# A convolution unit's banks read in halves, and the moments of the finished tiles in three pieces

## The reference, cut to what matters

```python
def _L1_xattn_ref(k, v, q, ssm_kernel, D, head_dim):     # k = v = ctx, q = layernorm(x)
    B, HD, L = k.shape
    H = HD // head_dim                                   # 32 heads of 8
    k_ = k.reshape(B, H, head_dim, L)
    v_ = v.reshape(B, H, head_dim, L)
    q_ = q.reshape(B, H, head_dim, L)
    kv = jnp.einsum('bhil,bhjl->bijhl', k_, v_)
    kv_f = jnp.fft.rfft(kv, n=fft_size)
    kernel_f = jnp.fft.rfft(ssm_kernel, n=fft_size)
    y = jnp.fft.irfft(kv_f * kernel_f, n=fft_size)[..., :L]
    out = y + kv * D[None, None, None, :, None]
    out = jnp.einsum('bijhl,bhil->bjhl', out, q_)
...
x = x + _L1_xattn_ref(ctx_2048, ctx_2048, _layernorm(x, axis=-1), L1_xattn_ssm_kernel, L1_xattn_D, 8)
x = x + _L1_ffn_ref(_layernorm(x, axis=-1), ...)
```

## Time and profile before

| | us |
|---|---|
| median of 3 timed runs | 2039.91 |
| lowest and highest | 2039.51, 2041.14 |
| the profiled execution | 2046.15 |
| its span | 2044.30 |
| TensorE busy in the span | 1912.9 (94%) |
| VectorE | 1396.4 (68%) |
| ScalarE | 802.7 (39%) |
| GpSimd | 641.8 (31%) |
| granted clock of TensorE, mean | 0.959 |

### The profile page before, as it was taken

One profiled execution on the slowest core, in us unless ns is written; L12 is line 12 of the kernel. 1 busy time (PEld: TensorE's weight loads), 2 busy tenths in 40 slices (PEclk: granted clock), 3 DMA queues, 4 the chain that ended last, 5 costly groups with the idle time before them and its releaser, 6 DMA issues. The chain is left out here.

```text
span 2044.3 us, 35178 instructions
## 1 busy us (share of the span) xinstructions
PE 1912.9 (94%) x13798; PEld 1629.1 (80%) x13798; DVE 1396.4 (68%) x2817; ACT 802.7 (39%) x1484; POOL 641.8 (31%) x507
## 2 busy tenths in 40 slices
PE   5799999999999999999999996999989989988997
PEld 3588888888888888999999995776777687767886
DVE  7778888888887866555555552788866847784554
ACT  5545555555455533122222212444534443232332
POOL 2433443333333330000000001776755620002553
PEclk6799999999999999999999997999999978998999
DMA  4211211111222133323223214535443443324774
GB/s 153 87 62 64 73 63 63 63 63 74 73 72 81 46 112 99 110 94 104 89 98 104 93 63 157 183 109 168 146 124 113 134 174 117 124 83 145 179 179 61
DMA packets 111752, 214.66 MB, mean 105 GB/s; under 512 B 14243, under 2 KB 34787, under 8 KB 110563
## 3 DMA queue, kind: packets, MB, share of 16 engines
q1 hardware_dynamic: 104194, 195.30, 28.4%
q0 software_dynamic: 7392, 17.11, 4.1%
HBM read 136.11 MB, written 76.34 MB: 104 GB/s over the span
## 5 line engine op out<-in xcount | busy, mean ns | idle before, releaser
L1415 PE MATMUL psum<-kv,toep 128*128 128x288 f32 x1280 | 328.3, 419 | 40.5 <-ACT yx L1463 24.3
L1415 PEld LDWEIGHTS psum<-kv,toep 128*128 128x128 f32 x1280 | 249.3, 196 | 117.0 <-ACT yx L1463 30.4
L168 PE MATMUL psum<-xn_t_h,w_gate_h 128*128 128x256 f32 x768 | 232.9, 303 | 1.3 <-DVE xn_th L293 1.3
L168 PE MATMUL psum<-xn_t_h,w_up_h 128*128 128x256 f32 x768 | 217.6, 283 | 0.0
L169 PE MATMUL psum<-xn_t_l,w_up_h 128*128 128x256 f32 x768 | 217.5, 283 | 0.0
L170 PE MATMUL psum<-xn_t_h,w_gate_l 128*128 128x256 f32 x768 | 217.5, 283 | 0.0
L169 PE MATMUL psum<-xn_t_l,w_gate_h 128*128 128x256 f32 x768 | 217.3, 283 | 0.0
L170 PE MATMUL psum<-xn_t_h,w_up_l 128*128 128x256 f32 x768 | 216.7, 282 | 0.0
L161 POOL TENSOR_TENSOR rstd<-rstd,minus_half 128x2 f32<-128x2 f32 x48 | 35.2, 733 | 520.3 <-DVE rstd L157 520.3
L276 ACT ACTIVATE xn_th<-psum 128x256 f32<-128x256 f32 x192 | 73.8, 384 | 312.1 <-PE psum L170 311.0
L1077 POOL TENSOR_SCALAR_AFFINE_SELECT operands<-operands 128x512 f32<-128x512 f32 x128 | 93.9, 733 | 320.9 <-ACT operands L820 320.9
(11 more groups left out here) (313 smaller groups left out, 4820.0 us busy)
## 6 DMA issues: line engine op xcount, KB each, us to landing
toep<-ssm_padded_scratch SPq DMA_DIRECT2D x64, 256.0 KB, 3.5
kx<-in_ctx_pairs SPq DMA_DIRECT2D x32, 384.0 KB, 4.4
x_scratch<-x_all SPq DMA_DIRECT2D x21, 512.0 KB, 2.8
x_all<-in_x SPq DMA_DIRECT2D x16, 512.0 KB, 3.8
operands<-in_ctx_t SPq DMA_DIRECT2D x16, 512.0 KB, 4.9
xn_t_scratch<-xn_t_h SPq DMA_DIRECT2D x16, 512.0 KB, 2.7
xn_t_scratch<-xn_t_l SPq DMA_DIRECT2D x16, 512.0 KB, 3.6
xn_t_h<-xn_t_scratch SPq DMA_DIRECT2D x16, 512.0 KB, 3.7
```

What stands on the lines that cost most here:

```text
L168: pe.run.matmul(out, lhs[0], rhs[0], start=first, stop=False)
L1415: ins = pe.run.matmul(out, w[:, (o - k) * P:(o - k + 1) * P], pairs, start=(k == 0), stop=(k == o))
```

## The change

Units that are followed by one turn of another kind and then by a unit (18, 26, 34, 38, 39, 42, 46, 47, 50, 58) are "halved": VectorE's near terms and ScalarE's copies are issued for the first two banks and then for the other two, each half with a signal. The unit two turns later starts when the first half has been copied, and waits for the second half before its third bank. The moments of tiles 0 to 5 are issued as two bn_stats behind unit n % 8 == 3, two behind n % 8 == 4, and the rest behind n % 8 == 5; GpSimd's inverse moves from n % 8 == 4 to 5 and ScalarE's normalise from 5 to 6. For tiles 6 and 7 nothing moves. The six load semaphores of the FFN's second weights become three, one for two pieces, and each wait is for both.

```diff
--- before.py
+++ after.py
@@ -402,7 +402,12 @@
                 xp = [us[:, :, :, :].rearrange("p t h c -> p t (h c)"), hsq[:, :, :, :].rearrange("p t h c -> p t (h c)"), x_t[2]]
                 xn3 = spare[:, 0:XB].rearrange("p (t d) -> p t d", t=ST)
                 xn3_t = [spare[:, (1 + i) * XB:(2 + i) * XB].rearrange("p (k n) -> p k n", k=KT) for i in range(2)]
-                stage2_loaded = [signal(f"stage2_loaded{i}") for i in range(len(stages2))]
+                pairs2 = [signal(f"stage2_pair{i}_loaded") for i in range(len(stages2) // 2)]
+                stage2_loaded = [pairs2[i // 2] for i in range(len(stages2))]
+
+                def pair_loaded_by(piece):
+                    return 16 * sum(loads_of(i) for i in range(piece // 2 * 2, piece // 2 * 2 + 2))
+
                 xt_loaded = [signal(f"xt_loaded{i}") for i in range(2)]
                 xp_moved = [signal(f"xp{i}_loaded_then_stored") for i in range(3)]
 
@@ -774,7 +779,7 @@
                             key = ("gate_up", B - 1, 0, JH - 1) if b < GH else ("down", B - 1, 0, ST - 1)
                             bank, filled, emptied, n = banks.at(*key)
                             act.wait_ge(filled, n + 1)
-                            act.wait_ge(stage2_loaded[b], loaded_by(b, len(stages2)))
+                            act.wait_ge(stage2_loaded[b], pair_loaded_by(b))
                             for src, parts_ in pieces2[b]:
                                 act.run.copy(parts_[0], src).then_inc(weight_high, 1)
                         elif name == "weights_high":
@@ -919,7 +924,7 @@
                             dve.settle(dve.run.memset(pad, 0.0))
                             dve.run.tensor_tensor(pad[:, P - 1:P], lag0[:, 0:1], dskip, ALU.add).then_inc(ssm_padded, 1)
                         elif name == "weights2":
-                            dve.wait_ge(stage2_loaded[b], loaded_by(b, len(stages2)))
+                            dve.wait_ge(stage2_loaded[b], pair_loaded_by(b))
                             for m, (src, parts_) in enumerate(pieces2[b]):
                                 dve.wait_ge(weight_high, SPLITS + splits_before(b) + m + 1)
                                 dve.run.tensor_tensor(parts_[1], src, parts_[0].bitcast(F32), ALU.subtract).then_inc(weight_low, 1)
@@ -1354,6 +1359,8 @@
             multiplied = signal("pairs_multiplied")
             convolved = signal("convolved")
             copied = signal("convolved_copied")
+            near_half = signal("near_terms_of_first_half_done")
+            copied_half = signal("first_half_copied")
             near_done = signal("near_terms_done")
             crossed = signal("crossed_terms_done")
             windowed = signal("query_windowed")
@@ -1385,6 +1392,13 @@
             set_of = {turn: i % 2 for i, turn in enumerate(turns)}
             before_of = {turn: (turns[i - 2] if i >= 2 else None) for i, turn in enumerate(turns)}
 
+
+            halved = [turns[i][1] for i in range(len(turns) - 2)
+                      if turns[i][0] == "unit" and turns[i + 1][0] != "unit" and turns[i + 2][0] == "unit"]
+
+            def halves(n):
+                return [slice(0, KB // 2), slice(KB // 2, KB)] if n in halved else [slice(0, KB)]
+
             def x_moved(r):
                 return (own_moved, 32 * r) if r < HT else (late_moved[r - HT], 0)
 
@@ -1399,7 +1413,10 @@
                 for turn in turns:
                     kind, n = turn
                     old = before_of[turn]
-                    if old and old[0] == "unit":
+                    split = kind == "unit" and old and old[0] == "unit" and old[1] in halved
+                    if split:
+                        pe.wait_ge(copied_half, halved.index(old[1]) + 1)
+                    elif old and old[0] == "unit":
                         pe.wait_ge(copied, old[1] + 1)
                     elif old:
                         pe.wait_ge({"tiles": tiles_added, "turn": rows_turned, "logits": logits_read}[old[0]], old[1] + 1)
@@ -1409,6 +1426,8 @@
                         pe.wait_ge(squared, g + 1)
                         pe.wait_ge(multiplied, g + 1)
                         for o in range(KT):
+                            if split and o == KT // 2:
+                                pe.wait_ge(copied, old[1] + 1)
                             out = bank_t[set_of[turn] * KT + o].rearrange("p (b c) -> p b c", c=64)[:, :, 0:NP_]
                             for k in range(o + 1):
                                 pairs = kv[g % 2][:, n % 2 * KB + k * HB:n % 2 * KB + (k + 1) * HB, :]
@@ -1457,10 +1476,15 @@
 
                 def copy_unit(n):
                     y = set_4d(("unit", n))
-                    act.wait_ge(near_done, n + 1)
                     act.wait_ge(crossed, n - 1)
-                    act.run.copy(yx[n % 2][:, :, 12:44], y[:, :, 0:4 * HR])
-                    act.run.copy(yx[n % 2][:, :, 0:12], y[:, :, 20:4 * HR]).then_inc(copied, 1)
+                    for part in halves(n):
+                        whole = part.stop == KB
+                        if whole:
+                            act.wait_ge(near_done, n + 1)
+                        else:
+                            act.wait_ge(near_half, halved.index(n) + 1)
+                        act.run.copy(yx[n % 2][:, part, 12:44], y[:, part, 0:4 * HR])
+                        act.run.copy(yx[n % 2][:, part, 0:12], y[:, part, 20:4 * HR]).then_inc(copied if whole else copied_half, 1)
 
                 def normalise(r):
                     act.wait_ge(row_norm_inverse, r + 1)
@@ -1476,7 +1500,7 @@
                         if n % 2 == 0 and n // 2 + 1 < NG_:
                             prepare(n // 2 + 1)
                         copy_unit(n)
-                        if n >= READY and n % 8 == 5:
+                        if n >= READY and n % 8 == 6:
                             normalise((n - READY) // 8)
                     elif kind == "turn":
                         act.wait_ge(rows_in_banks, n + 1)
@@ -1493,17 +1517,20 @@
                 def near_terms(n):
                     g = n // 2
                     y = set_4d(("unit", n))
-                    q = qx[g % 2][:, n % 2, :, :]
-                    f = terms[n % 2][:, :, :, :]
                     dve.wait_ge(convolved, n + 1)
                     dve.wait_ge(windowed, g + 1)
                     dve.wait_ge(summed, n - 1)
-                    dve.run.tensor_tensor(f[:, :, :, 0:4], y[:, :, 0:4 * HR].rearrange("p n (i d) -> p n i d", d=4),
-                                          window(q, 0, [[16, KB], [1, HR], [1, 4]]), ALU.mult)
-                    far = y[:, :, 4 * HR:NP_]
-                    dve.run.tensor_tensor(window(f, 4, [[HR * HR, KB], [4 * HR, 2], [HR, 4]]),
-                                          far.unsqueeze(2).broadcast_to([P, KB, 2, 4]),
-                                          window(q, 4, [[16, KB], [4, 2], [1, 4]]), ALU.mult).then_inc(near_done, 1)
+                    for part in halves(n):
+                        nk = part.stop - part.start
+                        q = qx[g % 2][:, n % 2, part, :]
+                        f = terms[n % 2][:, part, :, :]
+                        dve.run.tensor_tensor(f[:, :, :, 0:4], y[:, part, 0:4 * HR].rearrange("p n (i d) -> p n i d", d=4),
+                                              window(q, 0, [[16, nk], [1, HR], [1, 4]]), ALU.mult)
+                        far = y[:, part, 4 * HR:NP_]
+                        dve.run.tensor_tensor(window(f, 4, [[HR * HR, nk], [4 * HR, 2], [HR, 4]]),
+                                              far.unsqueeze(2).broadcast_to([P, nk, 2, 4]),
+                                              window(q, 4, [[16, nk], [4, 2], [1, 4]]), ALU.mult
+                                              ).then_inc(near_done if part.stop == KB else near_half, 1)
 
                 def sum_terms(n):
                     half, h = n // CH, n % CH
@@ -1521,12 +1548,14 @@
                         ins = dve.run.tensor_tensor(x[:, j, :], x[:, j, :], bank_t[set_of["tiles", r] * KT + j], ALU.add)
                     ins.then_inc(tiles_added, 1)
 
-                def statistics(r):
+                def tile_moments(r, js):
                     dve.wait_ge(tiles_added, r + 1)
-                    dve.wait_ge(row_normalised, r - 1)
-                    for j in range(BLK):
+                    for j in js:
                         ins = dve.run.bn_stats(bn[:, j, :], xl_of[r][:, j, :])
                     dve.settle(ins)
+
+                def statistics(r):
+                    dve.wait_ge(row_normalised, r - 1)
                     for j in range(BLK):
                         ins = dve.run.bn_aggr(mv[:, j, :], bn[:, j, :])
                     dve.settle(ins)
@@ -1539,7 +1568,9 @@
                         near_terms(n)
                         if n > 0:
                             sum_terms(n - 1)
-                        if n >= READY and n % 8 == 3:
+                        if n >= READY and n % 8 in (3, 4):
```

(5 more changed lines are left out.)

## The result

| | before | changed |
|---|---|---|
| median of 4 runs | 2040.38 | 2023.18 |
| lowest, highest | 2039.51, 2041.14 | 2022.38, 2025.16 |
| the profiled execution | 2046.15 | 2023.73 |
| its span | 2044.30 | 2021.4 |

The ratio is 0.9918, with a 95% interval from 0.9902 to 0.9934: 17 us less, in a range of 14 to 20. The spans differ by 22.9, more than the medians. TensorE's timeline tells why: the first tile turn, ahead of which the code is the same in both but for the pair signals, began at 1364.69 before and begins at 1359.82 now. These 4.9 us lie ahead of everything that was changed but the signals, and the signals alone did not move that start (1364.36, experiment 4).

The account below looks back on a forecast made before the run. TensorE's strict order bound the convolution stage, idling 24.3 us in 14 waits for ScalarE's second bank copy. Gains 6.4 + 5.6 + 5.5 + 2.6 = 20.1 us gave 2019.8 from a median of 2039.91, range 2013 to 2030.

Parts of the forecast that it names:

- The second wait goes: At U22 and its like, moments in three pieces free U20's banks before U21 ends, removing TensorE's wait (1.63 idle).
- A new wait of 1.15 at U24, U32 and U56 for the pair products: Blocks 0, 1 and 4: GpSimd's moved pow and product delay pair products; 1.15 replaces a 0.4 slip, bounds 0.4 and 2.
- 2.25 after the tile turn: Unit after each tile turn starts 2.25 after it instead of 3.45, by the halves: 1.2 us each, bounds 0 and 1.7.
- Around the row turns: Blocks with U38 and U46: U39 3.2 after its turn instead of 5.04, logits wait 0.9; gains 5.6 and 5.5 us.
- The last block: U62 starts 3.0 earlier, 0.4 given back because normalising precedes the row copies: 2.6 us won.
- Halves within a unit: Unit after a halved one: second half free at 3.2, TensorE needs it at 3.7, so that wait is covered.
- Signals: Waiting for both loads of a pair at the first casts costs 0, with over 40 us of cover.
- SyncE: Load queue: row store and x load wait for later normalising, Toeplitz load for U26 still lands in time; cost 0.
- The base: Whole kernel: profiled execution 2046.15 becomes 2026; the same 0.3% difference to the median gives 2019.8.
- The halves bring nothing: Rival, tile and row turns: a half costs as much as a whole, 10.2 us missing, 2030; chance 0.13.
- the clock falls: Rival: eleven remaining waits each bring a 1.2 GHz stretch of 1.5 to 2.6 us, at 2.6 giving 2048; chance 0.04.
- less is lost: Rival: GpSimd's move adds nothing to the 0.4, slow-clock stretches behind the logits go; 2013.4; chance 0.13.

Follow-up runs that it names:

- experiment 4: Kernel before with nothing but the three pair signals in place of six: ratio 1.0005 (0.9990 to 1.0020), stretch 279.7 us.
- the second trace: The changed kernel run once more, unaltered: ratio 0.9910 against the kernel before, 260.5 us from first tile turn to second row turn at the end.
- the later inverse: Changed kernel with GpSimd's inverse behind the pair products, normalising at n % 8 == 7, row store beside the x load: 2034.53 us, ratio 0.9960 to the kernel before.
- the first experiment: Changed kernel with moments, inverse and normalising back in their old places, halves and pair signals kept: 2035.99 us, ratio 0.9967 to the kernel before.

## Why the prediction was right, point by point

The time, 2023.2, lies in the range of 2013 to 2030, 3.4 above the 2019.8 named; the gain was 17.2 where 20.1 was worked out. The range is 17 us wide and would have held 2030 as well, the time without any gain of the halves; what bears the account out is the waits, one by one.

- **The second wait goes.** Right: U19 to U23 run without a gap.
- **A new wait of 1.15 at U24, U32 and U56 for the pair products, none in the other blocks.** Right in size (1.14, 1.14, 1.17), place and cause. U24 starts 28.25 after the tile turn where 27.80 was worked out, the 0.34 of the next point and 0.1 of scatter on.
- **2.25 after the tile turn: this term was mis-sized.** It is 2.59, which costs 0.34 in each of six blocks, 2.0 of the 2.3 us between the sum of 20.1 and the 17.85 of the stretch. The sizes of the half instructions were right or cautious (0.61 and 0.23 on VectorE, where 0.61 and 0.33 stood; ScalarE starts its copy 0.85 before U19, where 0.95 stood). The step that failed is the 0.03 between VectorE's end and ScalarE's start: it took ScalarE for free. I had named its preparation as what stands ahead of the copy at U38, and not at U18, U26 and their like, which are even units as well. Before, that preparation ended in time for the whole near terms (0.17 of idle in ScalarE's trace); when they are halved, it is late next.
- **Around the row turns.** The places are right: U39 3.05 after its turn (3.2), the logits at 30.71 (30.7), U40 at 34.30 (34.25). The wait of the logits shows as 0.45, counted from the modelled end of the last record; from U39's start and its pace of 4.88 it is 0.7, where 0.9 was worked out. Block 3 won 4.8 and not 5.5: its logits ran in 5.25 on the slower clock; in the second trace they did not. That the sums of 5.6 and 5.5 came out so well is partly luck: they rest on one trace of the kernel before, whose U39, U46 and work behind U47 ran slow. Against the trace of experiment 4 the changed kernel wins 4.6 in block 2, and in block 3 2.4 with its first trace and 4.0 with its second.
- **The last block**, 2.5 for 2.6. **Halves within a unit:** no wait before its third bank, five units in 24.52. **Signals:** 0. **SyncE:** 0 in the changed kernel, but how near that queue is to the path was shown by the later inverse: 3 to 4 us more delay of the row store and the x load made the start after a tile turn up to 2.4 us later. The prediction had looked at the Toeplitz load behind them and not at the pairs', which it should have.
- **The base.** The profiled execution came out at 2023.7 and not 2026: the profile of before had spent 4.9 us more ahead of the stretch, so its distance to the median was not the same in the changed kernel. That shift is no part of the gain.
- **The rivals.** "The halves bring nothing" falls with the first experiment, "the clock falls" with the pace of the units behind all waits up to 1.2, "less is lost" with the 1.14, and with the units behind the logits, which still ran slow (16.49 and 16.61).

## What to carry to other kernels

When a step is taken off the engine that frees a buffer, write down for every engine that the moved steps touch what they now stand in front of: here the pow on GpSimd, moved by one unit, stood ahead of work that TensorE needed, and of the 1.8 us won at the second wait 1.0 was given back in a plain block; putting it behind the pair products brought 1.4 there, more than the 0.86 of the halves. A shorter wait has a new last cause, so after sizing the halves ask again what ScalarE does at that moment; and a step that a store waits for also holds every load behind that store in the DMA queue, so loads that the next units need go first.

## What the runs showed of the hardware

The small VectorE step that writes less_mean behaves under crossed terms as under pair products: it lasts until GpSimd's instruction ends. In the changed kernel it starts at 1381.90 and takes 1.21, to 1383.11; GpSimd's crossed terms of that time end at 1380.98 + 2.10 = 1383.08.

```profile
1381.90 1.21 DVE L1562 TENSOR_SCALAR less_mean<-mv 128x4 f32<-128x4 f32 x1
```

The rule of the Trainium skill, page "SBUF — State Buffer", section "Who interferes with whom", that the two engines lock each other out of a shared port pair, agrees, for an instruction of four elements too. In which mode the step ran no run here shows.

The step behind it, which writes row_rstd, explains the longer second wait of the old order. It starts when the first pair product ends, and so does GpSimd's second pair product; in all 18 old-order blocks traced the two starts lie within 0.03. Mostly the step takes 0.16. In the others it lasts to the end of that product, as in block 3 of the kernel before: 1526.59 + 0.77 = 1527.36, and 1526.60 + 0.73 = 1527.33.

```profile
1526.59 0.77 DVE L1534 TENSOR_SCALAR row_rstd<-mv 128x4 f32<-128x4 f32 x1
1526.60 0.73 POOL L1565 TENSOR_TENSOR kv<-kx 128x256 f32<-128x256 f32 x1
```

This happened in 6 of the 18 blocks, and they are the six with a second wait of 2.23 to 2.25 instead of 1.63; with the moments in three pieces it happened in none of 60. It looks like a race that either engine may win, which the change took away; what decides it no run shows.

What I had not expected is how uncertain the clock is behind a wait of two to three microseconds. Behind waits up to 1.63 at a tile or row turn every unit of these traces ran at full pace. Behind longer ones it went either way, with nothing in the length to tell which: 2.10 and 2.11 full pace and 2.13 slow in one trace (three units in 16.48, granted clock 0.66 in the first 5 us, for 14.79 and 1.00); 2.23 to 2.25 full pace three times and slow three times; 2.49 full and 2.54 slow, twice each; 3.0 to 3.1 slow three times (U39 in the earlier trace rows and two tile turns of the later inverse) and full twice (experiment 4). A wait of 3.16 for a Toeplitz load at the start of the stage was followed by full pace as well. The pace of the logits differs between two traces of the changed kernel too: the second logits took 5.25 and 3.74, behind the same wait of 0.45. And the time ahead of the stretch, in code that none of the experiments on the units touches, ended anywhere from 1359.8 to 1369.9, with the waits for the first Toeplitz loads and the pace of the units between them; that may be a large part of what makes runs of one kernel scatter by 10 us, which no run here settles.
